# A relational graph layer on one core: one-hots handed over in pairs, and more of the gathers ahead of the scatters

## The reference

```python
h = jnp.maximum(_layernorm(x, axis=-1), 0.0)
row, col = (edge_index[0], edge_index[1])            # src, dst
deg = jax.ops.segment_sum(ones, row, num_segments=n)
deg_inv = jnp.where(deg > 0, jax.lax.rsqrt(jnp.maximum(deg, 1.0)), 0.0)
norm = deg_inv[row] * deg_inv[col]
h_j = h[col]
hj_b = comps[edge_type][:, :, None] * h_j[:, None, :]
msg = jnp.einsum('ebd,bdf->ef', hj_b, bases)
msg = msg * alpha[edge_type] * norm[:, None]
out = x + jax.ops.segment_sum(msg, row, num_segments=n)
```

## Time and profile before

| | us |
|---|---|
| median of 3 runs | 767.62 |
| the 3 runs | 767.0 to 768.07 |
| profiled execution | 762.65 |
| its span | 760.8 |

### The profile page before, as it was taken

How to read it: one execution, slowest core, us unless ns; L and a number is a source line. 1 busy time by engine, 2 the same in 40 slices (tenths; PEclk the granted TensorE clock), 3 DMA queues, 4 the chain that set the end, 5 groups by cost and what they waited for, 6 DMA issues and landing times. The chain is left out here.

```text
span 760.8 us, 13653 instructions
## 1 busy us (share of the span) xinstructions
PE 565.7 (74%) x3922; PEld 396.5 (52%) x3922; DVE 595.4 (78%) x2624; ACT 368.6 (48%) x1494; POOL 548.0 (72%) x404
## 2 busy tenths in 40 slices
PE   1999995566576886659769778777889669788860
PEld 0766654344354664446556556555666446554430
DVE  4999995578577897749879899869998869896630
ACT  0144346245343565455646565644566546465530
POOL 1788886344237777877888888888888778777875
PEclk9999997988798999999989999989999989999995
DMA  3899989989944545344444445435444534444332
GB/s 116 293 353 350 321 306 336 315 276 349 317 131 91 94 98 103 54 85 89 95 81 98 95 80 96 96 54 117 76 79 94 112 63 96 78 71 73 35 36 24
DMA packets 56527, 108.89 MB, mean 143 GB/s; under 512 B 9291, under 2 KB 48216, under 8 KB 55636
## 3 DMA queue, kind: packets, MB, share of 16 engines
q0 software_dynamic: 34496, 25.72, 25.0%
q1 hardware_dynamic: 5372, 55.14, 20.0%
q10 hardware_dynamic: 16584, 27.16, 11.6%
HBM read 94.89 MB, written 64.61 MB: 210 GB/s over the span
## 5 line engine op out<-in xcount | busy, mean ns | idle before, releaser
L389 POOL DMA_INDIRECT out_dram<-acc,scatter_idx x196 | 313.2, 1598 | 97.2 <-issue 43.7
L368 POOL DMA_INDIRECT rows<-in_x_dram,dst_i x196 | 232.8, 1188 | 107.5 <-issue 39.0
L723 PE MATMUL pst<-table_bits,turned_hot 128*128 128x198 f16 x1568 | 177.0, 261 | 79.4 <-DVE masked L476 63.4
L742 PE MATMUL pst<-bases_sb,h_turned 128*128 128x512 f32 x392 | 211.6, 623 | 0.0
L723 PEld LDWEIGHTS pst<-table_bits,turned_hot 128*128 128x128 f16 x1568 | 143.1, 103 | 106.4 <-issue 50.6
L513 DVE SCALAR_TENSOR_TENSOR part_sum<-pst,coef,part_sum 128x128 f32<-128x128 f32 x392 | 115.9, 344 | 104.7 <-ACT part_sum L636 100.2
L750 PEld LDWEIGHTS pst<-rows,same 128*128 128x128 f32 x392 | 71.3, 197 | 184.0 <-issue 160.5
L476 DVE SCALAR_TENSOR_TENSOR masked<-iota_h,lo,pst 128x198 f32<-128x198 f16 x392 | 141.7, 416 | 15.9 <-PE pst L723 8.7
L636 ACT ACTIVATE part_sum<-pst,coef 128x128 f32<-128x128 f32 x196 | 71.1, 363 | 154.2 <-PE pst L742 114.3
L750 PE MATMUL pst<-rows,same 128*128 128x128 f32 x392 | 83.5, 296 | 72.8 <-ACT acc L646 69.9
L646 ACT ACTIVATE acc<-pst,sum_scale 128x128 f32<-128x128 f32 x196 | 71.5, 365 | 81.9 <-DMA out_dram<-acc,scatter_idx 56.3
(11 more groups left out here) (71 smaller groups left out, 413.6 us busy)
## 6 DMA issues: line engine op xcount, KB each, us to landing
out_dram<-in_x_dram SPq DMA_DIRECT2D x50, 1000.0 KB
src_row<-src_rows ACTq DMA_DIRECT2D x25, 512.0 KB
edge_row<-edge_rows ACTq DMA_DIRECT2D x45, 256.0 KB
rows<-in_x_dram,dst_i POOLq DMA_INDIRECT x196
out_dram<-acc,scatter_idx POOLq DMA_INDIRECT x196
rows<-edge_rows ACTq DMA_DIRECT2D x10, 175.0 KB
edge_row<-edge_rows SPq DMA_DIRECT2D x4, 256.0 KB
src_row<-src_rows SPq DMA_DIRECT2D x2, 512.0 KB
```

What stands on the lines that cost most here:

```text
L368: pool.indirect_dma_start(row(t), None, x, bass.IndirectOffsetOnAxis(ap=dst_i[:, t:t + 1], axis=0)) \
L389: pool.indirect_dma_start(out, bass.IndirectOffsetOnAxis(ap=scatter_idx[:, t:t + 1], axis=0), acc[:, t % ACC_RING, :], None, compute_op=AL ...
L723: last = pe.matmul(pst[:, LOOK + t % 2, k * LO:(k + 1) * LO], turned_hot[:, g % 2, c, k * W + j * P:k * W + (j + 1) * P], table[:, c * LO: ...
L742: pe.matmul(pst[:, PRODUCT + t % 4, :], h_turned[:, g % 2, j, :], bases_sb[:].rearrange("d b f -> d (b f)"), start=True, stop=True).then_i ...
```

## The change

The semaphores between DVE and PE in the histogram count pairs of tiles instead of tiles. Each group of four gathers has a semaphore of its own, 49 of them, and the wait for statistics goes. The first 76 gathers (was 56) wait for the histogram, the pair of tiles t x 98 / 76. The waits for look-ups and products go, and so does all waiting for the gathers from 76 to 139, apart from the one of tile 115. After that two gathers go with five scatters, where seven went with ten: the last one stands ahead of scatter 140, where it stood ahead of scatter 154.

```diff
--- before.py
+++ after.py
@@ -66,7 +66,6 @@
     SAME_RING = 3 * BATCH
     PART_RING = 7
     ACC_RING = 6
-    GATHER_RING = 8
 
 
     def look_until(step):
@@ -79,11 +78,11 @@
 
     SUM_STEP, SUM_RATE = 3, 5
 
-    HIST_GATHERS, LOOK_GATHERS, FIRST_GATHERS = 56, 64, 88
+    HIST_GATHERS, FIRST_GATHERS = 76, 140
 
 
     def gathers_until(t):
-        return min(TILES, FIRST_GATHERS + (7 * t + 9) // 10)
+        return min(TILES, FIRST_GATHERS + 2 * t // 5)
 
     def sums_until(step):
         return min(TILES, GROUP * max(0, step), max(0, step - SUM_STEP + 1) * SUM_RATE)
@@ -235,7 +234,7 @@
         turned_hot_ready = sem("turned_hot_ready")
         look_ps = sem("look_ps")
         picked_ready = sem("picked_ready")
-        row_gathered = [sem(f"row_gathered{r}") for r in range(GATHER_RING)]
+        row_gathered = [sem(f"row_gathered{g}") for g in range(GROUPS)]
         row_summed = sem("row_summed")
         mean_ready = sem("mean_ready")
         row_squared = sem("row_squared")
@@ -350,24 +349,18 @@
 
             def pace(t):
                 if 0 < t < HIST_GATHERS:
-                    pool.wait_ge(hot_used, t * TILES // HIST_GATHERS)
-                elif HIST_GATHERS <= t < LOOK_GATHERS:
-                    pool.wait_ge(look_ps, (t - HIST_GATHERS + 1) * FIRST_LOOK * GROUP // (LOOK_GATHERS - HIST_GATHERS))
-                elif LOOK_GATHERS <= t < FIRST_GATHERS:
-                    pool.wait_ge(product_ready, (t - LOOK_GATHERS) // 2 + 1)
+                    pool.wait_ge(hot_used, t * HALF // HIST_GATHERS)
 
             def gather(t):
                 g = t // GROUP
-                if t % GROUP == 0 and g >= GATHER_RING:
-                    pool.wait_ge(row_squared, g - GATHER_RING + 1)
                 pace(t)
                 if t == EARLY_TILE:
-                    pool.wait_ge(hot_used, TILES)
+                    pool.wait_ge(hot_used, HALF)
                     pool.wait_ge(coef_ps, TYPE_PARTS)
                     pool.wait_ge(rows_stored, 16 * 4)
                 pool.indirect_dma_start(row(t), None, x,
                                         bass.IndirectOffsetOnAxis(ap=dst_i[:, t:t + 1], axis=0)) \
-                    .then_inc(row_gathered[g % GATHER_RING], 16)
+                    .then_inc(row_gathered[g], 16)
 
             pool.wait_ge(idx_ready, 1)
             for t in range(FIRST_GATHERS):
@@ -446,17 +439,19 @@
                 dve.tensor_scalar(type_hot[0:R, i % 2, :], type_row[0:R, i % TYPE_RING, :], chunk_id[0:R, 0:1], None,
                                   ALU.is_equal).then_inc(type_hot_ready, 1)
 
+
             for t in range(TILES):
-                if t >= HOT_RING:
-                    dve.wait_ge(hot_used, t - HOT_RING + 1)
+                if t >= HOT_RING and t % 2 == 0:
+                    dve.wait_ge(hot_used, (t - HOT_RING) // 2 + 1)
                 b = t % HOT_RING
                 dve.tensor_scalar(hots[:, b, 0:CHUNKS * P], iota_h[:], src_hi[:, t:t + 1], None, ALU.is_equal)
-                dve.tensor_scalar(hots[:, b, CHUNKS * P:], iota_h[:, 0:LO], lo[:, 1, t:t + 1], None,
-                                  ALU.is_equal).then_inc(hot_ready, 1)
+                last = dve.tensor_scalar(hots[:, b, CHUNKS * P:], iota_h[:, 0:LO], lo[:, 1, t:t + 1], None, ALU.is_equal)
+                if t % 2 == 1:
+                    last.then_inc(hot_ready, 1)
                 if t % TYPE_TILES == TYPE_TILES - 1:
                     type_hots(t // TYPE_TILES)
 
-            dve.wait_ge(hot_used, TILES)
+            dve.wait_ge(hot_used, HALF)
             for c in range(CHUNKS):
                 dve.tensor_scalar(table_bits[:, c * LO:(c + 1) * LO], pst[:, HIST + c, 0:LO], float(ONE), None,
                                   ALU.add).then_inc(table_ready, 1)
@@ -584,7 +579,7 @@
         @block.scalar
         def _(act):
             def stats(g):
-                act.wait_ge(row_gathered[g % GATHER_RING], 16 * GROUP * (g // GATHER_RING + 1))
+                act.wait_ge(row_gathered[g], 16 * GROUP)
                 for j in range(GROUP):
                     t = g * GROUP + j
                     last = act.activation(scratch[:, 0, j, :], row(t), ACT.Copy, accum_out=row_sum[:, t:t + 1])
@@ -704,11 +699,13 @@
 
             for t in range(TILES):
                 b = t % HOT_RING
-                pe.wait_ge(hot_ready, t + 1)
+                if t % 2 == 0:
+                    pe.wait_ge(hot_ready, t // 2 + 1)
                 for c in range(CHUNKS):
                     last = pe.matmul(pst[:, HIST + c, 0:LO], hots[:, b, c * P:(c + 1) * P], hots[:, b, CHUNKS * P:],
                                      start=(t == 0), stop=(t == TILES - 1))
-                last.then_inc(hot_used, 1)
+                if t % 2 == 1:
+                    last.then_inc(hot_used, 1)
                 if t % TYPE_TILES == TYPE_TILES - 1:
                     turn_types(t // TYPE_TILES)
```

## The result

Before: 767.31 us (764.4 to 768.07, 4 runs). Changed: 846.04 us (837.98 to 855.83, 4 runs). The ratio is 1.0999, interval 1.09 to 1.1098. The change makes the kernel 10% slower here; 735 us was predicted, and the range ended at 757.

A forecast was written before the change was run, and what follows sets the result against it. POOL was taken to set the pace from the first scatter on, with DVE's 9.96 us a step the floor once relieved. Terms 0 + 0 + 0 - 32.5 + 0 took the 767.6 us median to 735 us, range 708 to 757.

The forecast's parts named there:

- Histogram and hand-over by two: Histogram: halved waits between DVE and PE cost nothing, -2 to +1 us; the quicker gather pace alone brings nothing.
- The old pace by 56 was already faster than POOL: Histogram: POOL needs 1.91 us a gather, so about 52 gathers are out at 118 us before and after.
- Gathers behind the histogram: From 118 us: 88 gathers without waits take 113 us, first scatter at 231 us, x copies hidden, ending near 224.
- Steps 0 to 3: First four steps, 144.8 to 230.6 us before: 0 change, bounds 0 and +6 us for slower edge rows.
- Steps 4 to 12: Nine steps with two statistics groups in steps 4 to 11: 122 us against 121.3; bounds -11 and +27 us.
- Steps 13 to 40, and tail: Steps 13 to 40: 10.4 us a step instead of 11.56, 32.5 us less; tail of 38 scatters: 0, down to -5.
- The sum: Whole kernel: 0 + 0 + 0 - 32.5 + 0, profiled execution from 762.65 to 730.1 us, median 735 us.
- D': Behind the histogram: each gather packet waits for one copy packet, 65 us late, 789 us; chance 0.01.
- C: Steps 4 to 11: two statistics groups hurt as in steps 0 to 3, 37 us more, median 772 us; chance 0.05.
- D: Behind the histogram: gathers crowd the queue, the first scatter lands 22 us later, 746 us; chance 0.07.
- the port rule: Beside the histogram: GpSimd and VectorE share an exclusive port pair, so GpSimd's descriptors wait; quicker pace alone brings nothing.

The follow-up runs named there:

- e1: Kernel before with only the one-hots handed over by two tiles, its gathers unchanged; 762.73 us, ratio 1.0001, chip 11.
- h3: Changed kernel with the one-hots handed over tile by tile again, gathers as changed; 849.48 us, ratio 1.106, chip 0.
- h4: Changed kernel with an always-met wait added to each of gathers 76 to 139; 853.45 us, ratio 1.1111, chip 0.
- h2: Changed kernel, gathers 76 to 83 waiting for look-ups, 84 to 139 for products, one statistics group a step from step 4; 771.47 us, chip 0.
- i2: Changed kernel, every fourth gather from 76 to 139 waiting until the four before have landed; 818.24 us, ratio 1.0641, chip 6.
- f1: The changed kernel itself, unedited, run again on chip 5; 746.28 us, ratio 0.9762 to the kernel before.
- g1: The changed kernel itself, unedited, run on chip 6; 850.47 us, ratio 1.1063 to the kernel before.
- g3: Changed kernel with one group of statistics a step instead of two from step 4 on; 822.26 us, ratio 1.0696, chip 6.
- i3: The changed kernel itself, unedited, run again on chip 6; 850.40 us (843.59 and 857.21), 1.107 by the medians.
- i1: Changed kernel, 112 gathers before scatters: 56 paced by histogram, 8 by look-ups, then three a product; one statistics group a step from step 4; 750.11 us, chip 6.
- e4: Changed kernel with gathers 76 to 83 waiting for look-ups and 84 to 139 for products; 747.93 us, ratio 0.9789, chip 11.
- f2: Changed kernel with an always-met wait added to each of gathers 76 to 139; 743.32 us, ratio 0.9723, chip 5.
- f4: Changed kernel with 88 gathers ahead of the scatters and seven with ten behind, as before; 765.14 us, ratio 1.0013, chip 5.
- g2: Changed kernel with nothing to pace its first 115 gathers; 899.28 us, ratio 1.1698, chip 6.
- h1: Changed kernel with nothing to pace its first 115 gathers, run on chip 0; 904.05 us, ratio 1.177.

## Why the prediction was wrong

**Histogram and hand-over by two.** Priced at -2 to +1 us. True of the hand-over (e1 against before; h3 has the loss without it). The quicker pace was another matter: with it the table began 20.4 us late in the first comparison, 14.6 in h4 and some 42 in h2 and i2, but 0 to 2 us late in f1, g1, g3, h3 and i3, though up to gather 76 h4 and i2 are the same program as g1 and i3. POOL had 58 gathers out at 110 us where it had 47, by gathers of 0.95 us issued while DVE stood. "The old pace by 56 was already faster than POOL" holds while DVE is busy; once DVE stands, POOL is fast enough to keep it standing. That a pace of 56 would hold it back then, and 76 doesn't, is my explanation and not shown: the two traces with 56 on a chip of this kind, before and i1, were on time (112.8 and 114.0 us), but so were four of the eight with 76.

**Gathers behind the histogram.** This is the step that failed. Their own cost was right: 1.27 us each for 1.285 forecast, the 140th issued at 223.95 us, and the copies' end fell at some 210 us, well hidden. What was missing was what they do to others, and the prediction put that at nothing. I asked whether the row of gathers delays the first scatter and never what an unbroken POOL does to PE's signals. The cost is the +78.9 us from the table to the first product, more than twice the forecast gain. "I take 0 for steps 0 to 3, with bounds 0 and +6" left out the stretch ahead of step 0 altogether; no term of the sum covered it. The remote waits of 1.97 and 3.52 us at 119 and 125 us, in the trace of before, were the only warning, and they stand where the row of gathers was longest. They don't give the size: the row there is broken after a few gathers, and one of 84 us is outside of what that trace has.

**Steps 0 to 3.** Off by -4.4 us on the first chip, since the gathers are over by then, but +12.1 us on chip 5 (97.9 against 85.8), where some 70 gathers lie beside them. In f1 DVE waits 14.2 us there for edge rows to land. The bound of +6 named a cause that is there (before waits 0.4 us for edge rows in these steps) and was too small.

**Steps 4 to 12.** 122 us forecast, 138.1 measured, 136.3 on chip 5, inside the bound of +27. The mechanism was right and the size off: 12.7 us was set for a step with two groups, 2.7 over DVE's own, and g3 shows that the second group alone costs 4.

**Steps 13 to 40, and tail.** Right: 10.44 us a step for 10.4, DVE busy 274.3 of 292.2 us, 94%. POOL's gaps ahead of scatters grew as said, from 38.6 to 61.9 us, but not for the reason given: the landing of an earlier scatter ended 26.2 us of them, ACT's acc only 12.5. The tail took 71.8 us, at the -5 us bound.

**The sum.** On chip 5 it reads -5.5 us ahead of step 0 (139.3 for 144.8), +12.1, +15.0, -31.8, -4.4: -14.6, and the span is 746.0 for 760.8. The median of 746.28 us lies inside the range, and the gain in steps 13 to 40 is the one forecast; beside its own before the kernel gains 18.3 us there, not 32.5, because steps 0 to 12 take half of it back. On the first chip -31.6 is outweighed by +99.3.

**The rivals.** None held the mechanism, and none reached 846 us; the slowest, D', was put at 789. C, the case that ended slower, had its price from the two groups of statistics, which came to 16.8 of the 37 us that it feared in steps 4 to 12 (step 1 of before took 18.9 us, not the 18.5 given there). D looked at the right place, the crowd of gathers, and priced only the data's queue: from 142 to 226 us the changed kernel's DMA engines still moved 274 GB/s, and POOL issued gathers at its own pace. D', the one gather packet for one of the copies, is refuted: from 142 to 206 us, while the copies last, 1619 gather packets went beside 571 of theirs. Of the port rule cited from the Trainium skill, "SBUF — State Buffer", section "SBUF: two separate sides", the trace agrees as to POOL: its gathers took 0.95 us wherever DVE stood, and 1.6 us beside the histogram. Not every work of DVE slows them, though: beside the look-ups of f1, with DVE busy 55 of 84 us, one took 0.99 us. The same section says that PE never waits on another engine's port. No row here speaks of ports, but whoever reads from it that POOL can't hold up PE's exchange is refuted by i3 and i1, at least 843.59 against 750.11 us on one chip.

## What to carry over

An engine that issues descriptors without a break can cost others their signals: when taking waits out of such a row, price it as a row that gets longer, and search the trace of before for waits that no instruction accounts for, however short. Keep a wait for fresh work of another engine every three or so of such instructions; a wait that is already met is no break. And before explaining a surprising time by parts of the edit, run the unedited changed kernel again beside them, best on another chip: seven experiments here (e1 to e4, f2 to f4) ran where the effect did not show.

## What was not expected of the hardware

- The same program takes 744.9 to 747.7 us on chip 5, and 838.0 to 857.2 us on chip 6 and in the first comparison (its chip is not on record), while the kernel before differs by 0.7% (762.81 to 768.16 us). I call chips 0 and 6 one kind and 5 and 11 the other, which is a reading: only chip 6 was used twice, with chip 0 between, and both times it showed the loss. That a chip changes with time, or that something else differed between the groups, is not excluded, and what the difference is isn't known. Nor is it known whether a denser row would do the same on chips 5 and 11, because g2 and h1 did not fall on one.
- On the one kind a signal of PE mostly gets through once in about 22 us while POOL issues a gather every 1.26 us (20.98 and 21.56 us in g2, up to 21.8 in g1; but 32.0 once in i2 and 55.4 once in h1), and about 1 us into POOL's pause in the rows of i2. Signals of DVE to PE aren't late: PE starts 0.8 us behind the pick. Nor is it the signal alone: in h1 DVE had a pair of one-hots ready at 38.3 us, and PE, waiting for nothing that the profile shows, started the pair's eight matmuls over 10.5 us, where a pair otherwise takes 1.5 us. PE's timeline of h1, four of its seven rows there:

```profile
38.35 0.51 PE L705 MATMUL pst<-rows 128*128 128x198 f16 x2 [2.70 <-issue]
...
43.03 0.32 PE L705 MATMUL pst<-rows 128*128 128x198 f16 x1 [1.77 <-issue]
...
46.71 0.32 PE L705 MATMUL pst<-rows 128*128 128x198 f16 x1 [1.94 <-issue]
48.81 0.32 PE L705 MATMUL pst<-rows 128*128 128x198 f16 x1 [1.78 <-issue]
```

DVE still waited until 93.74 us. So there PE's own work is held up too, which a signal that only travels late would not do; what holds it, and whether anything but gathers does it, was not settled.
- In the histogram it may feed itself: while DVE stands a gather takes 0.95 us instead of 1.6, which makes the row denser.
- The delay lasts on for 9 us in the changed kernel (232.85 after 223.95) and 15 in g1 behind the last gather's issue, in g1 with no engine and no DMA at work. So something that had piled up seems to be drained; what that is, no run here shows.
